# Attention kernel on one core: products for maxima by pairs and sums over keys by three products in the last slots

## What is computed

```python
h = _layernorm(x)                                     # x: (16, 512, 512)
mod = jax.nn.silu(time) @ mod_w + mod_b               # time = cond[:, None, :]
shift, scale, gate = jnp.split(mod, 3, axis=-1)
h = h * (scale + 1.0) + shift
qkv = (h @ w_qkv).reshape(B, T, 3, H, e).transpose(2, 0, 3, 1, 4)   # H = 16, e = 32
q, k, v = (qkv[0], qkv[1], qkv[2])
q = _apply_rope(_layernorm(q, q_norm_w), position)
k = _apply_rope(_layernorm(k, k_norm_w), position)
scores = jnp.einsum('bhqe,bhke->bhqk', q, k) / jnp.sqrt(jnp.asarray(e, q.dtype))
attn = jax.nn.softmax(scores, axis=-1)
o = jnp.einsum('bhqk,bhke->bhqe', attn, v)
return x + o.transpose(0, 2, 1, 3).reshape(B, T, D) @ w_out * gate
```

## Time and profile before

| | |
|---|---|
| median of 3 runs | 1695.15 us (1694.68 to 1695.43) |
| the profiled execution's own time | 1697.0 us |
| its span | 1694.8 us |
| mean granted TensorE clock over the span | 0.986 |
| TensorE busy | 1633.6 us, 96% |
| VectorE, ScalarE, GpSimd busy | 1238.2, 997.5, 977.5 us |

### The profile page before, as it was taken

One profiled execution on the slowest core, in us unless ns is written; L12 is line 12 of the kernel. 1 busy time (PEld: TensorE's weight loads), 2 busy tenths in 40 slices (PEclk: granted clock), 3 DMA queues, 4 the chain that ended last, 5 costly groups with the idle time before them and its releaser, 6 DMA issues.

```text
span 1694.8 us, 31070 instructions
## 1 busy us (share of the span) xinstructions
PE 1633.6 (96%) x11846; PEld 960.7 (57%) x11846; DVE 1238.2 (73%) x1541; ACT 997.5 (59%) x1484; POOL 977.5 (58%) x769
## 2 busy tenths in 40 slices
PE   5979999999999999999999999999999999999887
PEld 3745565565555556566556555555656655655344
DVE  8767777777777777777777777777777777776453
ACT  3436665666666656566566666665656656666552
POOL 0525466566666665656656666666665665666452
PEclk9979999999999999999999999999999999999899
DMA  6024455546546455555555555654645555454563
GB/s 219 26 62 94 107 124 116 137 110 145 116 104 153 109 125 128 125 118 119 138 115 128 128 122 117 133 125 109 147 113 118 132 118 136 108 122 103 125 137 106
DMA packets 55417, 204.25 MB, mean 121 GB/s; under 512 B 6872, under 2 KB 6872, under 8 KB 39144
## 3 DMA queue, kind: packets, MB, share of 16 engines
q0 software_dynamic: 18144, 132.13, 38.6%
q1 hardware_dynamic: 37128, 70.14, 13.0%
HBM read 53.25 MB, written 16.88 MB: 41 GB/s over the span
## 4 chain that ended last, share of the span: by engine, by line
PE 91%; DVE 4%; issue 1%; ACT 1%; DMA 1%; SPq 0%; POOL 0%; DVEq 0%; ACTq 0%
PE Y L339 33%; PE O L447 13%; PE SA L428 13%; PE Y L357 10%; PE SM L396 6%; PE MB L379 3%; PE SA L432 3%; PE Y L462 3%; PE SA L331 2%; DVE cst L1053 1%; PE SA L406 1%; ACT probs L806 1%; DMA probs<-in_L_cond_w_qkv_dram 1%; DMA probs<-probs 1%; DVE wqkv_lo L1096 0%
## 5 line engine op out<-in xcount | busy, mean ns | idle before, releaser
L1288 POOL TENSOR_TENSOR probs<-probs 128x2048 f32<-128x2048 f32 x62 | 285.4, 4603 | 313.3 <-DMA probs<-probs 313.3
L1053 DVE TENSOR_REDUCE cst<-SM 128x2 fp32r<-128x1024 f32 x256 | 313.9, 1226 | 144.4 <-PE MB L396 142.6
L806 ACT ACTIVATE probs<-SM 128x1024 f32<-128x1024 f32 x256 | 263.0, 1027 | 137.9 <-PE SM L432 123.2
L1053 DVE TENSOR_REDUCE cst<-MB 128x2 fp32r<-128x1024 f32 x256 | 311.5, 1217 | 0.0
L808 ACT ACTIVATE probs<-SA 128x1024 f32<-128x1024 f32 x256 | 260.2, 1016 | 0.0
L447 PE MATMUL O<-probs,vals 128*32 128x512 f32 x2048 | 255.3, 613 | 0.0
L339 PE MATMUL Y<-wqkv_hi,hT_lo 128*128 128x512 f32 x716 | 225.5, 410 | 0.4 <-DVE hT_lo L1037 0.4
L1261 POOL TENSOR_TENSOR pair_part<-rows,rope_pair 128x256 f32<-128x256 f32 x128 | 120.3, 940 | 169.4 <-DVE rows L1031 168.5
L339 PE MATMUL Y<-wqkv_hi,hT_hi 128*128 128x512 f32 x716 | 213.4, 420 | 0.0
L715 ACT ACTIVATE rows<-Y 128x512 f32<-128x512 f32 x121 | 72.4, 598 | 221.1 <-PE Y L339 221.1
L339 PE MATMUL Y<-wqkv_lo,hT_hi 128*128 128x512 f32 x716 | 201.5, 403 | 0.0
(11 more groups left out here) (221 smaller groups left out, 3448.5 us busy)
## 6 DMA issues: line engine op xcount, KB each, us to landing
probs<-probs POOLq DMA_DIRECT2D x126, 1024.0 KB, 7.1
xin<-in_x_dram SPq DMA_DIRECT2D x62, 256.0 KB, 2.6
xres<-in_x_dram SPq DMA_DIRECT2D x60, 256.0 KB, 2.6
out_dram<-xres SPq DMA_DIRECT2D x60, 256.0 KB, 5.8
shift_scale<-mod_rows SPq DMA_DIRECT2D x15, 512.0 KB, 3.7
gate<-mod_rows SPq DMA_DIRECT2D x16, 256.0 KB, 3.2
rows<-in_L_cond_mod_w_dram SPq DMA_DIRECT2D x2, 1024.0 KB, 9.0
probs<-in_L_cond_w_qkv_dram SPq DMA_DIRECT2D x2, 1024.0 KB, 13.1
```

Of the source, the lines that this page charges most:

```text
L806: act.activation(a[:, 2:4, :], SM[:], ACT.Exp).then_inc(s_exp, 1)
L1053: dve.tensor_reduce(heads[:, 2 * half:2 * half + 2, 0], (SM, MB)[half][:], AX.X, ALU.max, negate=True).then_inc(max_out, 1)
L1288: pool.tensor_tensor(total, total, part, ALU.add).then_inc(keys_summed, 1)
```

## The change

It has two parts, both from slot 58 on, and moves some calls.

1. In slots 58 to 62 `scores_by_query` is replaced by `scores_by_pair`: two matmuls for heads 0 and 1, and later two for heads 2 and 3, both into the two MB banks. Each pair waits for the maximum of the pair before. `qm_count` numbers the pairs for VectorE. SM isn't used for it, and `scores_by_key` waits for a maximum in its first tile alone.
2. For groups 58 to 62 `add_part` makes the sum over keys by three products with ones that accumulate in one bank: buffer 3 as it is, buffer 0 with 1 added by the one DMA that is left, buffer 2 as it is. `sum_keys` and the second DMA addition are gone for them. ScalarE waits on `part_summed` before it writes over a summed buffer.

Moved: in slot 62 `project_out` of tile 57 goes from the second tile's step to the third's, with its gate and its residual; `project_out` in the fourth step is cut 4 and 8 around the second pair; in slots 59 to 62 `output_high` stands ahead of `high_qk` on ScalarE.

```diff
-        def qm_bank(i):
-            return SM[:, i, :] if i < 2 else MB[:, i - 2, :]
+
+        def qm_bank(g, i):
+            return MB[:, i % 2, :] if late(g - 1) else SM[:, i, :] if i < 2 else MB[:, i - 2, :]
+
+
+        def qm_count(g, t, pair):
+            whole = min(g, SPLIT)
+            return TT * whole + 2 * TT * (g - whole) + (2 * t + pair + 1 if late(g - 1) else t + 1)
...
+            def scores_by_pair(g, t, pair):
+
+                n = TT * g + t
+                if t == 0 and pair == 0:
+                    pe.wait_ge(qk_low, 2 * g + 2)
+                pe.wait_ge(max_out, 2 * n + pair)
+                cols = slice(t * P, (t + 1) * P)
+                for i in (2 * pair, 2 * pair + 1):
+                    r = head_rows(i)
+                    mm = pe.matmul(qm_bank(g, i), qk_hi[r, g % 2, 0, cols], qk_hi[r, g % 2, 1, :],
+                                   start=True, stop=True)
+                mm.then_inc(qm_done, 1)
...
@@ -415,7 +438,7 @@
                         pe.wait_ge(h_lo, 6)
                 if n > 0:
                     pe.wait_ge(s_exp, 2 * n)
-                if t == 0 or group(g + 1):
+                if t == 0 or not late(g):
                     pe.wait_ge(max_out, 2 * (n + TT - 1) + 1)
...
             def add_over_keys(g, bank):
 
-                if g < LAST - 1:
-                    pe.wait_ge(keys_summed, g + 1)
-                else:
+                pe.wait_ge(keys_summed, g + 1)
+                for i in range(HG):
+                    mm = pe.matmul(bank[head_rows(i), :], ones_r[:, 0:E].bitcast(F32),
+                                   probs[:, probs_buffer(g, 2), i, :], start=True, stop=True, skip_group_check=True)
+                mm.then_inc(ones_done, 1)
+
+            def add_part(g, m, bank):
+
+                t = (3, 0, 2)[m]
+                pe.wait_ge(s_exp, 2 * (TT * g + t) + 2)
+                if t == 0:
                     pe.wait_ge(first_added, 16 * (g + 1))
-                    pe.wait_ge(second_added, 16 * (g + 1))
-                parts = (2,) if g < LAST - 1 else (0, 2)
-                for t in parts:
-                    for i in range(HG):
-                        mm = pe.matmul(bank[head_rows(i), :], ones_r[:, 0:E].bitcast(F32),
-                                       probs[:, probs_buffer(g, t), i, :],
-                                       start=(t == parts[0]), stop=(t == 2), skip_group_check=True)
-                mm.then_inc(ones_done, 1)
+                for i in range(HG):
+                    mm = pe.matmul(bank[head_rows(i), :], ones_r[:, 0:E].bitcast(F32),
+                                   probs[:, probs_buffer(g, t), i, :],
+                                   start=(m == 0), stop=(m == 2), skip_group_check=True)
...
@@ -555,6 +583,9 @@
                 scores_by_key(s, 0)
                 if late(s - 1):
                     weigh_values(s - 1, 3)
+                if s == LAST:
+                    add_part(s - 1, 0, MB[:, 1, :])
+                    add_part(s - 1, 1, MB[:, 1, :])
                 if s > 0 and tile(s + 4):
                     if s > 1:
                         pe.wait_ge(sum_ln, s - 1)
@@ -565,24 +596,37 @@
                 begun = 5 if s > 0 and not late(s - 1) else 0
                 if begun:
                     project_part(s + 4, 2, Y[:], 0, begun)
-                if group(s + 1):
+                if late(s) and group(s + 1):
+                    scores_by_pair(s + 1, 0, 0)
+                    if tile(s + 4):
+                        project_part(s + 4, 2, Y[:], begun, 9)
+                        begun = 9
+                    scores_by_pair(s + 1, 0, 1)
+                    if late(s - 1) and not tile(s + 4):
+                        pe.wait_ge(y_gated, n)
+                        add_part(s - 1, 0, Y[:])
...
                 scores_by_key(s, 1)
                 if late(s):
-                    weigh_values(s, 0)
                     if group(s + 1):
-                        scores_by_query(s + 1, 1)
+                        scores_by_pair(s + 1, 1, 0)
+                        if late(s - 1) and tile(s + 4):
+                            pe.wait_ge(v_out, s + 5)
+                            add_part(s - 1, 0, Y[:])
+                        weigh_values(s, 0)
+                        scores_by_pair(s + 1, 1, 1)
+                        if late(s - 1):
+                            add_part(s - 1, 1, Y[:])
+                        if s == LAST - 1:
+                            add_part(s - 1, 2, Y[:])
                     else:
+                        weigh_values(s, 0)
                         add_last_sums(0)
-                        add_over_keys(s - 1, MB[:, 1, :])
-                    if s == LAST - 1:
-
-                        pe.wait_ge(o_low, n + 1)
-                        pe.wait_ge(y_gated, n)
-                        project_out(n, Y[:], 0, 12)
+                        add_part(s - 1, 2, MB[:, 1, :])
...
                 scores_by_key(s, 2)
                 if late(s):
                     if group(s + 1):
+                        scores_by_pair(s + 1, 2, 0)
                         weigh_values(s, 1)
-                        scores_by_query(s + 1, 2)
-                        if tile(s + 4):
+                        scores_by_pair(s + 1, 2, 1)
+                        if s == LAST - 1:
+
+                            pe.wait_ge(o_low, n + 1)
+                            pe.wait_ge(sum_ln, s)
+                            project_out(n, Y[:], 0, 12)
+                        elif late(s - 1):
+                            add_part(s - 1, 2, Y[:])
+                        else:
                             pe.wait_ge(v_out, s + 5)
-                        pe.wait_ge(y_gated, n + 1 if s == LAST - 1 else n)
-                        add_over_keys(s - 1, Y[:])
+                            pe.wait_ge(y_gated, n)
+                            add_over_keys(s - 1, Y[:])
                     else:
...
                 scores_by_key(s, 3)
                 if late(s):
-                    weigh_values(s, 2)
                     if group(s + 1):
-                        scores_by_query(s + 1, 3)
+                        scores_by_pair(s + 1, 3, 0)
+                        weigh_values(s, 2)
                         m = n + 1 if s == LAST - 1 else n
                         pe.wait_ge(o_low, m + 1)
-                        pe.wait_ge(sum_ln, s)
-                        project_out(m, Y[:], 0, 12)
+                        if s == LAST - 1:
+                            pe.wait_ge(y_gated, m)
+                        else:
+                            pe.wait_ge(sum_ln, s)
+                        project_out(m, Y[:], 0, 4)
+                        scores_by_pair(s + 1, 3, 1)
+                        project_out(m, Y[:], 4, 12)
                     else:
+                        weigh_values(s, 2)
                         add_last_sums(2)
...
@@ -786,6 +844,9 @@
                     if g > 0 and t == 0:
                         act.wait_ge(pv_step, TT * (g - 1) + 2)
                         act.wait_ge(first_added, 16 * g)
+                    elif late(g - 1) and t < 3:
+                        act.wait_ge(pv_step, TT * g)
+                        act.wait_ge(part_summed, 2 * (g - 1 - (NT - 6)) + t)
...
                 move_c(s)
+                if late(s - 1) and s < LAST:
+                    output_high(s - 5)
                 if group(s + 1):
                     high_qk(s + 1, 0)
                     high_qk(s + 1, 1)
                 key_exponentials(s, 0, 0)
-                if late(s - 1) and s < LAST:
...
-                if s > 0 and (s == LAST or not late(s)):
+                if s > 0 and (s >= LAST - 1 or not late(s)):
                     log_sums(s - 1, Y[:] if s < LAST else MB[:, 1, :])
                 key_exponentials(s, 2, 0)
                 key_exponentials(s, 2, 1)
-                if late(s) and s < LAST:
+                if late(s) and s < LAST - 1:
                     log_sums(s - 1, Y[:])
...
-                dve.wait_ge(qm_done, TT * g + t + 1)
+                dve.wait_ge(qm_done, qm_count(g, t, half))
...
-                dve.tensor_reduce(heads[:, 2 * half:2 * half + 2, 0], (SM, MB)[half][:], AX.X, ALU.max, negate=True
+                bank = MB if half or late(g - 1) else SM
+                dve.tensor_reduce(heads[:, 2 * half:2 * half + 2, 0], bank[:], AX.X, ALU.max, negate=True
...
-                if s == LAST - 1:
-                    apply_gate(s - 5, Y[:], gated[:])
                 if tile(s + 5):
                     inverse_roots(s + 7)
                     normalize_qk(s + 5)
                 if group(s + 1):
                     maxima(s + 1, 2)
+                if s == LAST - 1:
+                    apply_gate(s - 5, Y[:], gated[:])
...
-                if s > 0:
+                if s > 0 and not late(s - 1):
                     sum_keys(s - 1)
                 add_keys(s, 1)
-                if s - 5 >= 0 and not late(s) or s == LAST - 1:
```

(17 more changed lines are left out.)

1 line of the change is left out of this document (added).

## The result

The changed kernel takes 1699.01 us (median of 9 runs, 1698.58 to 1704.88), the kernel before 1695.15 us (9 runs, 1692.67 to 1698.21). The ratio is 1.0033 with a 95% interval of 1.0025 to 1.0041: slower by a third of a per cent. The profiled execution took 1699.01 us, with a span of 1697.2 us.

What follows compares the result with a forecast made beforehand. TensorE's in-order stream was taken as the bound. Terms +0.8, +0.7, +0.4, +3.7 and -1.3 sum to +4.3 us, giving 1701.3 us profiled and 1699.4 as median; range 1690.5 to 1704.5.

Steps and rivals of the forecast that it cites:

- What bounds the kernel: TensorE's in-order stream sets the end, busy 1633.6 of 1694.8 us; a query tile's step is a ring of 4.35 us.
- The product of a pair: Two matmuls for maxima hold TensorE 0.44 us, as long as four; the bank is free 1.92 us after the start.
- Rival 2: Not slower: a pair costs half, 0.22 us, saving 8.8 us over 20 tiles, so 1690.6 us; chance 0.18.
- Slot 58: First projected slot, priced with pairs and three products with ones: 21.6 us against 20.79, +0.8.
- The third tile's first pair 1.92 after 10.16: In slot 58, that pair was placed 1.92 us after 10.16 us into the slot, on the way to 21.6.
- Slots 60 and 61: Slots without V's projection: 22.2 us each at full clock, 44.4 against 43.96 together, +0.4.
- Edit 2: Sums over keys by three products: nine more products with ones, 8.6 us of TensorE, all counted in the steps.
- Edit 3: Slot 62 with the projection of tile 57 moved later: 25.9 us against 22.16, +3.7, with a wait for o_lo.
- Slot 63: No DMA wait (0.81 us before); third tile's scores reached after 8.88 us against 10.22, -1.3.
- The clock: The changed kernel runs at 1.00, while the kernel before lost some 4.8 us to 1.2 GHz in slots 59 to 61.
- a clock under 0.95 in several slots: One of the signs named beforehand that would show the forecast wrong.
- rival 1: The clock stays as it was in the late slots, returning 4.8 us: +9.1, 1704.2 us, slower; chance 0.24.

Runs made afterwards that it cites:

- two kernels that keep the old sums: The kernel before with seven unused products added (1690.99 us), and the kernel before with only the products by pairs (1696.10 us).
- the filler: Kernel before plus seven products whose results are never used, in TensorE's gaps of slots 58 to 62: 1690.99 us, ratio 0.9981.
- the pairs alone: Kernel before with only the products for maxima by pairs; sums over keys and slot 62's order as before: 1696.10 us, ratio 1.0004.

## Why the prediction was right, and where its steps were not

The time (1699.4 forecast, 1699.01 measured) and the sign came as forecast, but that the number is this close is in part luck. The steps were priced some 4.7 us too high over the six slots; a wait of 1.66 us on VectorE and 2.7 us of lost clock (1.49 in slot 58, 1.18 in slot 60), which the sum did not have, made up for it. Slot 62 was forecast as the largest loss and is one of the two; slot 58, the other, was not. Nor did the 1.85 us carry over by which the profiled execution of before lay above its median: 1701.3 was forecast for the profiled one, and it took 1699.01, the median itself.

- **What bounds the kernel.** Right: TensorE's stream, with a ring through VectorE. The changed kernel waits for a maximum 12 times in slots 58 to 62, 8.5 us in all.
- **The product of a pair.** Right at the end that was taken: the next work starts 0.43 us behind a pair (1619.65 to 1620.08), as it starts 0.44 behind a product of four. Rival 2 is out. The price depends on the neighbours, though: a pair that stands behind scores by key takes 0.33 us (1622.11 to 1622.44). The interval was a bit high: the bank is free after 1.82 us, or 1.72 for a pair that stands behind scores by key, not 1.92. Scores by key to a pair take 1.03 us, not 1.14. Each makes the steps shorter: slot 61 takes 21.12 us where 22.2 was forecast, and slot 59 22.57 instead of 23.3.
- **Slot 58.** The step that failed. "The third tile's first pair 1.92 after 10.16" counts the maxima of VectorE and nothing else. The 2.35 us of roots and normalisation that its queue holds between them, covered before, lengthened the wait there from 0.33 to 1.99 us, and the clock fell behind it, which took another 1.49. Moving them away took slot 58 to 20.68 us, with the work of tile 63 then paid in slot 59; so at full clock the pairs themselves cost nothing in slot 58, where +0.8 was forecast.
- **Slots 60 and 61.** +0.4 forecast, -0.54 measured. Slot 60 took 22.30 us, close to the 22.2 forecast, but by luck: at a clock of 0.92, not at 1.00. At full clock such a slot of the changed kernel takes 21.12 us, 1.06 more than the 20.06 of before; it gains only because the kernel before ran them at 0.78 and 0.92. The 1.06 us come from the first tile, 1.3 us longer (1.45 forecast); the second and third are 0.2 us shorter each, where 0.12 longer was forecast.
- **Edit 2.** The products with ones were priced as all paid. Beside pairs that is right for most of their time: slot 61 takes 21.12 us with three products and 19.80 with one, 1.3 of the 1.9 us priced. Behind products of four they are hidden in the gap of 1.42 us. The price of a part depended on the other part.
- **Edit 3.** The wait for o_lo came as worked out, 1.01 us for 0.9, and the slot at 25.05 us for 25.9. But that was not "a step that was covered": 0.56 us of the wait already stood in the earlier trace rows, and with products of four the same order costs 0.4 us. The pairs cost 2.5 us there, of which the longer wait for o_lo is 0.5.
- **Slot 63.** Right in its length: 8.83 us for 8.88 to the third tile's scores, no wait for a DMA. But the 1.3 us were credited to the three products, and 1.1 of them also come in two kernels that keep the old sums; the wait that was to be saved does not stand in every execution.
- **The clock.** "I let the changed kernel run at 1.00" was half right: 1.00 in slots 59, 61 and 62, 0.93 and 0.92 in slots 58 and 60. Slot 60 took 1.2 us more than slot 61 for it. By the prediction's own signs this one speaks against it: "a clock under 0.95 in several slots" came in two of the five, so rival 1 was half right. That the clock had cost the profiled execution of the kernel before some 4.8 us is borne out: with the gaps filled slots 59 to 61 took 4.1 us less, and 0.7 more would have gone without the waits for exponentials in slot 61. That execution was a long one (1697.0 us against a median of 1695.15); by the medians the filler gives back 2.9 us.

So the change is slower because the ring of two maxima in one pair of banks takes 3.5 to 3.6 us a tile. Where nothing stands between two pairs, in the first tile, TensorE waits it out and then still has the product with ones to do, and in slot 58 VectorE has no room left for the work of tile 63. Its other half, the products with ones, pays for itself only without the pairs. The Trainium skill (page "TensorE: Matmul & The Clock Gate", section "A second HAM failure mode: psum-queue depth-cycling") tells of a kernel in which short idling between groups of matmuls that cycle through the PSUM banks makes the clock swing between its two levels. It decided nothing in the forecast; the filler agrees with it: with the gaps of 1.42 us filled, slots 59 to 61 ran at 1.00 instead of 0.92, 0.78 and 0.92.

## What to carry to other kernels

When an engine waits in a ring that two buffers close, work that fits into the wait is free, and the same work beside a tightened ring is mostly paid: price the parts of a change together and apart. Before a ring is tightened, list everything in the queue of the engine that closes it, not only the operations of the ring. And where the granted clock falls in stretches with short regular waits, look at what can stand in the waits, before anything is taken out of them.

## What the runs showed of the hardware

Adding seven products that nothing uses, about 6.8 us of TensorE work at 0.97 us each, made the kernel 3 us faster, because slots 59 to 61 then ran at 2.4 GHz throughout (62.43 us for 66.49). Gaps of 1.42 us that came back once or twice a slot were followed by falls to 1.2 GHz in some executions; in slots 59 to 62 of the profiles with filled gaps, where 0.4 to 0.6 us were left of most, there was none. The changed kernel's clock fell in slots 58 and 60 behind waits of 1.99 and 1.32 us, but not in slots 61 and 62 behind 1.33 us, nor did that of the pairs alone in slots 60 and 61 behind 1.32. That leaves open what exactly the chip reacts to. Much of the scatter of the kernel before, 1691 to 1698 us over all its runs, goes with it, as the runs at a clock of 0.990 and of 0.987 or less above show: with the gaps filled the runs of one kernel lie within 1.4 to 3.4 us.

Two matmuls on two groups of 32 rows held TensorE as long as four on four groups, 0.43 against 0.44 us to the next kind of work. From a pair to the moment when its two banks are free again it took 1.82 us, of which VectorE's maximum is 1.23.
